# A chunked delta-rule recurrence on one core: the state's update moved into its own round, the old state's reads into the last level, and the copy that starts XT one level earlier

## The reference, cut to what matters

```
mem = DECAY * mem + sdt
sur = sigmoid(SBETA * (mem - THR)); hard = mem > THR; spike = hard (in value)
mem = mem - spike * THR
alpha = sigmoid(abt + alpha_spike * spike)       # 1 where no channel fired
beta = sigmoid(bbt + sum(spike * beta_spike)) * active
s = s * alpha
u = kt @ s
s = s - beta * outer(kt, u) + beta * outer(kt, vt)
out = s.T @ qt
```

## Time and profile before

| what | value |
|---|---|
| time, median of 3 runs | 1432.69 us (1431.52 to 1444.1) |
| the profiled execution: time / span | 1437.39 us / 1435.7 us |
| mean granted TensorE clock | 0.893 |
| busy, share of span | PE 83%, PE weight loads 57%, DVE 51%, ACT 36%, POOL 14% |

### The profile page before, as it was taken

The page is one execution under the profiler, slowest core; times in us unless marked ns, Lnnn a source line. Parts: engine busy times, 40 slices in busy tenths (PEclk is TensorE's granted clock), DMA queues, the critical chain, the costliest instruction groups (busy, mean ns, idle before and its releaser), DMA issues. The chain is left out here.

```text
span 1435.7 us, 41273 instructions
## 1 busy us (share of the span) xinstructions
PE 1197.7 (83%) x17200; PEld 824.4 (57%) x17200; DVE 735.1 (51%) x2526; ACT 519.8 (36%) x1455; POOL 204.8 (14%) x390
## 2 busy tenths in 40 slices
PE   2599966899999999999999988587997798799778
PEld 1112113777777787777888876346455444644554
DVE  4746554777777776777766652126124212612421
ACT  2434311134443344344444444144225324421532
POOL 4100021012112111221122221202001100200110
PEclk9979865599999999999999999689998998999899
DMA  2000000000000000000000000300000000000000
GB/s 73 0 1 0 1 0 0 3 3 3 3 3 4 3 4 3 3 4 3 3 4 4 4 4 3 120 8 1 0 15 0 0 7 7 0 0 15 0 0 7
DMA packets 11733, 11.40 MB, mean 8 GB/s; under 512 B 1532, under 2 KB 9840, under 8 KB 11568
## 3 DMA queue, kind: packets, MB, share of 16 engines
q1 hardware_dynamic: 11567, 9.01, 2.1%
HBM read 7.96 MB, written 1.05 MB: 6 GB/s over the span
## 5 line engine op out<-in xcount | busy, mean ns | idle before, releaser
L849 PE MATMUL banks<-work 64*64 64x32 f32 x2048 | 89.1, 229 | 35.7 <-DVE work L701 33.1
L849 PEld LDWEIGHTS banks<-work 64*64 64x64 f32 x2048 | 78.9, 145 | 65.5 <-issue 54.2
L986 ACT COPY work<-banks 128x128 f32<-128x128 f32 x160 | 42.8, 267 | 194.0 <-PE banks L839 194.0
L696 DVE TENSOR_TENSOR work<-work,banks 128x128 f32<-128x128 f32 x128 | 36.9, 289 | 148.3 <-PE banks L849 148.2
L859 PE MATMUL banks<-work 64*64 64x32 f32 x2560 | 111.0, 227 | 0.5 <-issue 0.4
L809 PE MATMUL banks<-work 64*64 64x64 f32 x3072 | 104.9, 240 | 7.2 <-DVE gates L691 6.5
L839 PE MATMUL banks<-work,gates 64*64 64x32 f32 x2560 | 110.5, 226 | 0.0
L305 DVE SCALAR_TENSOR_TENSOR gates<-mom,gates 128x16 f32<-128x16 f32 x512 | 103.3, 202 | 10.8 <-ACT gates L396 6.1
L839 PEld LDWEIGHTS banks<-work,gates 64*64 64x64 f32 x2560 | 97.5, 143 | 10.2 <-issue 9.9
L309 DVE SCALAR_TENSOR_TENSOR mom<-gates 128x16 f32<-128x16 f32 x512 | 99.9, 195 | 6.0
L859 PEld LDWEIGHTS banks<-work 64*64 64x64 f32 x2560 | 101.3, 148 | 0.9 <-issue 0.6
(11 more groups left out here) (226 smaller groups left out, 2475.2 us busy)
## 6 DMA issues: line engine op xcount, KB each, us to landing
work<-in_x_dram SPq DMA_DIRECT2D x5, 256.0 KB, 2.9
out_dram<-work SPq DMA_DIRECT2D x4, 256.0 KB, 2.3
gates<-in_w_ff_dram SPq DMA_DIRECT2D x3, 256.0 KB, 4.8
wv_sb<-in_wv_dram SPq DMA_DIRECT2D x1, 512.0 KB, 4.5
work<-in_w_out_dram SPq DMA_DIRECT2D x1, 512.0 KB, 4.9
gates<-in_x_Wq_dram SPq DMA_DIRECT2D x1, 512.0 KB, 6.3
gates<-in_x_Wk_dram SPq DMA_DIRECT2D x1, 512.0 KB, 6.9
gates<-in_x_Wv_dram SPq DMA_DIRECT2D x1, 512.0 KB, 7.8
```

The source lines that it names most:

```text
L849: last = pe.matmul(packed(psZX, l)[rows, hp], XT[rows, n.two, hp], first_half(Z[:, l - 1], l)[rows, hp], start=True, stop=True)
L986: ac.copy(first_half(Z[:, l - 1], l), packed(psZX, l)).then_inc(z_ok, 1)
```

## The change

Four moves within the bodies; no instruction is added, removed or changed in shape. VectorE: the update of the state goes from level 1 of the next body to its own body, ahead of `alpha`. TensorE: the two reads of the old state go from behind level 5 into level 5, on both sides of `write_state`. ScalarE: `start_xt(aft)` goes from the end of level 5 to level 4, ahead of `keep_out`; `fade(cur)` goes from the end of the body into level 5, ahead of `soft_alpha` and `copy_start`.

```diff
@@ VectorE, body
                         spike(scan, h + 1)
-                        if l == 1 and prev:
-                            update(prev, 0)
-                            update(prev, 1)
                         if aft:
                             prefix(aft, l)
...
                     spike(scan, 6 * NINV)
+                    if cur:
+                        update(cur, 0)
+                        update(cur, 1)
                     if gate:
                         alpha(gate)
@@ TensorE, body
                             if l == 5:
+                                read_state(cur, 0)
                                 write_state(cur)
+                                read_state(cur, 1)
...
-                    if cur:
-                        read_state(cur, 0)
                     if aft:
                         turn_start(aft)
                     if cur:
-                        read_state(cur, 1)
                         read_chunk(cur)
@@ ScalarE, body
                             keep_u(cur)
+                        if l == 4 and aft:
+                            start_xt(aft)
                         if l == 4 and prev:
                             keep_out(prev)
+                        if l == 5 and cur:
+                            fade(cur)
                         if l == 5 and gate:
                             soft_alpha(gate)
-                        if l == 5 and aft:
-                            start_xt(aft)
                     if aft:
                         copy_start(aft)
-                    if cur:
-                        fade(cur)
```

## The result

The changed kernel takes **1389.25 us** (median of 5 runs, 1388.88 to 1403.12) against 1432.69 (5 runs, 1428.14 to 1444.1): a ratio of 0.9706, 95% interval 0.9647 to 0.9765. The profiled execution is the longest of the five, 1403.12 us with a span of 1401.4. The same kernel was profiled a second time among the experiments: 1386.28 us with a span of 1384.5.

A forecast was written before the change was run, and what follows sets the result against it. Neither TensorE nor VectorE is full; they wait on each other, and clock falls add 26.4 us. Profiled 1437.4 - 24.6 (path) - 24.0 (clock) = 1388.8; the median, 4.7 below that execution, gives 1384 us, range 1374 to 1415.

The forecast's parts named there:

- The path at the body's end: Level 5 to the next body's start: `prefix(aft, 5)` 0.14 us later, `level(aft2, 0)` 0.58 earlier, VectorE's idle 0.90 absorbing the update.
- 0.86 us a round: Rounds with scan at full clock: `prefix(aft, 1)` and `make_x(2)` come 0.86 us earlier; 20 rounds give 17.2 us.
- GpSimd's place: GpSimd's steps fall beside other steps of VectorE than before: priced at nothing, 0.2 us a round either way.
- The clock: Scan rounds: a shorter TensorE wait ahead of `make_x(2)` ends all but one clock fall, gaining 24 of 26.4 us.
- Bodies without scan: Eight bodies without scan gain 0.80 us each, 6.4 us together, with the granted clock 1.00 from 705 to 890 us.
- the drain: Four bodies at the end, where the pipeline drains and there is less to push back: about 1 us gained.
- 18.3 us for a round: Sign in the profile after: ScalarE's `keep_res` every 18.3 us in the bodies with scan.
- a clock of 1.00 to the end of the rounds: Sign in the profile after: granted clock 1.00 from about 310 us to the end of the rounds.
- 1 (falls stay): The clock keeps falling in every second round, leaving only the rounds' gain, about 22 us: 1411 us, chance 0.18.
- 3 (TensorE held at the first read): Level 5: `read_state(cur, 0)` waits for ScalarE's `keep_out`, from about 1.05 us no gain, more falls: 1458 us, chance 0.06.
- 4 (the update waits for `fade`): Body's end: `fade` ends no sooner, the update waits ahead of `alpha`, level 1's gain is lost: 1433 us, chance 0.05.

The follow-up runs named there:

- before_fill_keys_first: Kernel before with `turn_ks`'s eight transposes issued twice and GpSimd's `keys(aft2)` moved ahead of `root(prev)`: 1432.73 us, ratio 1.001.
- alpha_first: Kernel after with VectorE's update behind `alpha` instead of ahead of it: 1409.17 us, ratio 0.985 to the kernel before.
- both kernels filled: Kernel before and kernel after, each with `turn_ks`'s eight transposes issued twice, same result: 1401.75 us (ratio 0.983) and 1379.70 us (0.963).

## Why the prediction was right

- **The path at the body's end: right.** Taken to the frame of the earlier trace rows (add 52.69): the first read at 608.66 (forecast 608.57), `prefix(aft, 5)` 610.54 (610.50), the update 612.23 (612.19), `prefix(aft2, 0)` 613.22 (613.10), `beta_sums` 613.36 (613.23), `add_x(1)` 615.12 (614.99), `prefix(aft, 1)` 615.71 (615.53), `make_x(2)` 617.44, 0.67 earlier than before (forecast 0.86). Of the 0.12 at `prefix(aft2, 0)` 0.09 is a slip of the walk, which had `alpha` end at 613.19 and `prefix` start at 613.10 behind it. The reads and `write_state` overlapped better than reckoned (`level(aft, 5)` 609.66, not 609.97), which nobody waited for.
- **0.86 us a round: mis-sized, 1.31 measured.** The walk itself gave 0.67 in the round shown and 0.80 in most (0.43 to `add_x(1)`, 0.37 from there to `make_x(2)`), a little less than forecast. The rest, 0.51, comes between `make_x(2)` and `make_x(3)`, 3.32 us before and 2.81 after. That is the term of GpSimd's place, which I priced at nothing with 0.2 either way. Twenty rounds by 1.31 are 26.2 us, not 17.2.
- **The clock: right in kind and nearly in size.** Forecast 24 of 26.4 us. Scan rounds take 364.8 and 361.4 us in the two executions, 20 by 17.86 are 357.2, so 7.6 and 4.2 us are left for falls and uneven rounds: 19 to 22 gained. That it was the wait ahead of `make_x(2)` is shown from both sides: filled in the kernel before, the falls went; put back in the kernel after, some came back; and within before_fill_keys_first they follow the long waits alone. It isn't the whole rule: at the same 0.77 the kernel after has one or two falls and alpha_first five.
- **Bodies without scan: right by path, wrong in sum.** At full clock some take 17.0 to 17.2 (17.9 before), the 0.80 forecast. But they now see falls, three in one execution and one in the other, where I took the clock as 1.00 as before. The 7.4 us forecast for them and the drain became a loss of 6.4 and a gain of 0.8. Where the clock was kept up nearly throughout (both kernels filled) the gain was 4.4, 183.0 to 178.6. What brings the clock down there is open: in the first execution the fall at 757 us follows a wait of 0.78 us that the profile puts down to nothing, one of 0.48 and one of 0.46, and such a wait isn't there in every body (ahead of the fall at 802 us of the second execution the same three are 1.08, 0.48 and 0.60):

```profile
753.98 0.13 PEld L809 LDWEIGHTS banks<-work 64*64 64x64 f32 x1 [0.78 <-issue]
...
755.13 0.54 PEld L849 LDWEIGHTS banks<-work 64*64 64x64 f32 x16 [0.48 <-ACT work L985]
756.13 0.35 PEld L809 LDWEIGHTS banks<-work 64*64 64x64 f32 x16 [0.46 <-issue]
```

- **Why the sum came out at 1384 against 1389 nevertheless:** errors against each other. The gain was put 9 us too low for the path of the scan rounds, 7 to 14 too high for the late bodies, and 2 to 5 too high for the clock; the stages outside the rounds added 4 us in one execution and took 2 in the other. The mechanism holds, but that the sum came within 5 us is in part luck. Of the signs named, 18.3 us for a round (17.86) and a clock of 1.00 to the end of the rounds (0.98 and 0.92) did not come true.
- **Rivals.** 1 (falls stay) is what the reads alone did. 3 (TensorE held at the first read) didn't happen. 4 (the update waits for `fade`) is what the update alone does, 0.90 us; the moved reads are what make room for it. In that sense the parts need each other: alone they gave 1.3% and nothing, together 2.9%. With the clock kept up by filling in both kernels, the whole change is worth 22 us by the medians (1401.75 to 1379.7) and 28 by the ratios (0.983 to 0.963), of which the profiled rounds show 18.6; so of its 43 us the path is about half, and the rest is the clock.

## What to carry to other kernels

Ask of a shortened path what it does to the waits of TensorE that remain: a move that shortened the round by 0.77 us gained nothing since the clock fell oftener, and 16 useless matmul instructions a round gained 1.7%. Before working on the path, look at the granted clock by stretches, find the wait that stands ahead of a fall, and fill it by hand as a test. An update that nobody needs for four rounds belongs where its engine is idle, but what it waits for has to be moved ahead first.

## What the runs showed of the hardware that I had not expected

Two groups of matmuls of half the array each, the reads of the old state (8 instructions each), overlapped with the full group between them: from the first read's loads (555.97) to those of `level(aft, 5)` (556.97) it took 1.00 us, where I had added up 1.40. A step of VectorE of 0.18 us took 0.71 beside a GpSimd product of 0.73, and one of 0.44 that takes its data from PSUM took no longer. And the clock over equal work isn't the same from execution to execution: the same kernel at the same full-clock round of 17.86 us had granted clocks of 0.92 and 0.97 in its late bodies, and took 1403.1 and 1386.3 us; 7.3 of these 16.9 us lie in the late bodies.
